# Transposes of q, k, p and x1 moved from TensorE to the DMA queue, in a transformer block with an LSTM

## The reference

```python
def cond(x, image):                      # causal attention, 16 heads of 16, one more key per sequence
    q, k, v = split(x @ c_attn_w + c_attn_b, 3)
    k = concat([image @ uk_w.T + uk_b, k]); v = concat([image @ uv_w.T + uv_b, v])
    p = softmax(where(causal, q @ k.T / sqrt(16), -10000) + mask)
    return (p @ v) @ c_proj_w + c_proj_b
def attn(y):                             # linear attention, relu on q and k, no softmax
    q, k, v = relu(y @ Wq.T + bq), relu(y @ Wk.T + bk), y @ Wv.T + bv
    out = (q @ (k.T @ v)) / max(q @ sum(k), 1e-6)
    return layernorm(out + y) * gamma + beta
x1 = x + attn(cond(x, image))
h  = lstm(x1, h0=image)                  # 64 steps over the tokens, 256 wide, gates 4 x 256
out = x1 + fp4_linear(silu(fp4_linear(h, w_gate)) * fp4_linear(h, w_up), w_down)
```

## Time and profile before

| | us |
|---|---|
| median of 3 runs | 1017.58 |
| lowest, highest | 1013.61, 1018.38 |
| the profiled execution | 1014.53 |
| its span, first to last instruction | 1012.4 |
| busy: TensorE, its weight loads | 866.5, 579.3 |
| busy: VectorE, ScalarE, GpSimd | 805.1, 495.7, 346.8 |

### The profile page before, as it was taken

The page is one execution under the profiler, slowest core; times in us unless marked ns, Lnnn a source line. Parts: engine busy times, 40 slices in busy tenths (PEclk is TensorE's granted clock), DMA queues, the critical chain, the costliest instruction groups (busy, mean ns, idle before and its releaser), DMA issues.

```text
span 1012.4 us, 27497 instructions
## 1 busy us (share of the span) xinstructions
PE 866.5 (86%) x9798; PEld 579.3 (57%) x9798; DVE 805.1 (80%) x2157; ACT 495.7 (49%) x1177; POOL 346.8 (34%) x436
## 2 busy tenths in 40 slices
PE   3359887988989898988977899999999999999984
PEld 1246655666666666666654565565665665666642
DVE  6388999778777877788764688888888888888884
ACT  2264656666676667666653333433343433333431
POOL 0053667555555556555642011111111111111111
PEclk9588999999999999999999999999999999999997
DMA  4600011011001110111010000000000000000001
GB/s 108 197 13 21 19 37 33 22 36 34 27 24 34 34 31 20 34 34 33 17 31 17 1 12 21 22 21 21 17 17 21 21 22 21 19 14 22 21 22 26
DMA packets 41239, 30.36 MB, mean 30 GB/s; under 512 B 12082, under 2 KB 40050, under 8 KB 41173
## 3 DMA queue, kind: packets, MB, share of 16 engines
q1 hardware_dynamic: 41172, 29.42, 10.3%
HBM read 20.87 MB, written 8.54 MB: 29 GB/s over the span
## 4 chain that ended last, share of the span: by engine, by line
PE 39%; DVE 23%; issue 13%; ACT 5%; POOL 2%; DVEq 1%; POOLq 0%; ACTq 0%
PE bank L713 14%; PE bank L882 8%; PE bank L981 6%; PE bank L871 6%; DVE hqT L1533 3%; PE bank L973 3%; ACT hqT L1183 2%; DVE kv_bd L1381 2%; DVE pT L458 2%; ACT qk L1054 1%; DVE h_value L170 1%; DVE qk L1375 1%; PE bank L718 1%; DVE prob L1323 1%; DVE v L1394 1%
## 5 line engine op out<-in xcount | busy, mean ns | idle before, releaser
L665 POOL TENSOR_TENSOR ffn_room<-h_value,h_scale 128x704 f32<-128x704 f32 x32 | 44.4, 1388 | 291.7 <-DVE h_value L171 291.7
L713 PE MATMUL bank<-gu,xqT 128*128 128x512 f16 (+1 forms) x576 | 128.2, 362 | 1.3 <-DVE xqT L1548 1.3
L613 POOL TENSOR_TENSOR p<-prob,p 128x520 f16<-128x520 f32 x64 | 80.5, 1258 | 68.4 <-ACT p L1065 68.3
L882 PE MATMUL bank<-wh,h 128*64 128x512 f16 x768 | 100.2, 385 | 3.5 <-ACT h L1158 2.1
L871 PE MATMUL bank<-wx,x1T 128*64 128x512 f16 x768 | 93.8, 379 | 0.9 <-DVE x1T L441 0.9
L772 PE MATMUL bank<-ident,p 128*65 128x128 f16 x1024 | 76.0, 223 | 16.5 <-ACT qT L1119 9.9
L981 PE MATMUL bank<-dn,hqT 128*128 128x256 f16 x576 | 70.3, 278 | 20.7 <-DVE hqT L1533 20.7
L1148 ACT ACTIVATE sig<-bank 128x256 f32<-128x256 f32 x64 | 24.8, 388 | 127.2 <-PE bank L882 126.6
L871 PEld LDWEIGHTS bank<-wx,x1T 128*64 128x64 f16 x768 | 78.9, 202 | 11.2 <-DVE x1T L441 1.2
L713 PEld LDWEIGHTS bank<-gu,xqT 128*128 128x128 f16 x576 | 53.7, 98 | 53.6 <-issue 9.9
L606 POOL TENSOR_TENSOR prob<-prob,row_max 128x520 f32<-128x520 f32 x64 | 68.5, 1089 | 37.0 <-DVE row_max L1331 36.8
(11 more groups left out here) (199 smaller groups left out, 2064.0 us busy)
## 6 DMA issues: line engine op xcount, KB each, us to landing
x_in<-in_x_columns SPq DMA_DIRECT2D x32, 128.0 KB, 2.2
x_res<-in_x SPq DMA_DIRECT2D x32, 128.0 KB, 2.1
x_rows<-x_rows_sb SPq DMA_DIRECT2D x32, 128.0 KB, 1.9
ffn_room<-x_rows SPq DMA_DIRECT2D x64, 64.0 KB, 2.2
out<-ffn_room SPq DMA_DIRECT2D x64, 64.0 KB, 2.0
mask_in<-in_mask_Bx1x1xS_ff SPq DMA_DIRECT2D x64, 16.0 KB, 2.4
x1T<-in_L_cond_Wx SPq DMA_DIRECT2D x1, 1024.0 KB, 6.5
x1T<-in_L_cond_Wh SPq DMA_DIRECT2D x1, 1024.0 KB, 8.5
```

The costliest lines, as they stand in the source:

```text
L613: pool.tensor_tensor(p16[:, 1, r, :], prob[:, r, :], p16[:, 0, r, :], ALU.subtract).then_inc(s["p_lo"], 1)
L665: pool.tensor_tensor(blocks(hq, FF), blocks(fp4_h.value, FF), spread(fp4_h.scale, FF), ALU.mult).then_inc(s["hq_ready"], 1)
L713: last = pe.matmul(dst, lhs(a, c), rhs(b, c), start=first and c == 0 and a == b, stop=c == C - 1 and (a, b) == parts3[-1], skip_group_chec ...
L882: last = pe.matmul(bank[e][B * h:B * h + B, :], h16[:, m, c, :], half_cols(wh16, a, c, h), start=False, stop=True, skip_group_check=True)
```

## The change

- q and k are transposed by two DMAs (64 rows x 2048 values each), p by two (128 rows x 1024 values, 8 heads each), x1 by one (128 rows x 512 values, high and low). The DMAs are issued by SyncE, in its list. The copies from PSUM behind TensorE's transposes go, and so do those transposes.
- p is laid out so that a head's 64 high and 64 low values become the 128 partitions of its transpose. v stands on the partitions twice, so one product gives high and low: 32 products in `attend` for 64. v is made twice by TensorE, for each sequence and each half of the partitions.
- The image key is left out of the transposed p. GpSimd multiplies its weight by the image's values (`image_part`), and VectorE adds that to the sums. The image's values come per tile as broadcast rows by two DMAs.
- All masks are loaded once, 1 MB, ahead of the first tile.
- x1's high and low parts are made from rows, by ScalarE and GpSimd, before they are transposed.
- `hold` is a wait as an instruction of its own, followed by the increment of a semaphore that nobody reads.
- The lists of all engines are reordered. Scores of the two halves use banks 0 to 3, one pair each.

The diff, cut to its core:

```diff
 def qkv(t):
...
-            after(pe, s["x1T_lo"], t.count(back=5))
-            lhs = lambda a, c: xT16[:, a, P * c:P * c + P]
-            for dst, lo, hi in ((bank[2], 0, 2 * D), (bank[1][:, 0:D], 2 * D, 3 * D)):
...
+            after(pe, s["masked"], t.count(2, 2, back=1))
+            bias(bank[2], "attn", 0, 2 * D)
+            product(bank[2], lambda a, c: xT16[:, a, P * c:P * c + P], lambda b, c: attn16[:, b, c, 0:2 * D], False)\
+                .then_inc(s["qk_ps"], 1)
+            row = bias_bf["attn"][:, None, 2 * D:3 * D].to_broadcast([96, 2, D])
+            pe.matmul(bank[3], ones_bf[:, :], row, start=True, stop=False, skip_group_check=True)
+            for h in range(2):
+                for c in range(C):
+                    for a, b in parts3:
+                        for copy in range(2):
+                            last = pe.matmul(bank[3][64 * copy:64 * copy + 64, D * h:D * h + D],
+                                             xT16[:, a, P * c + 64 * h:P * c + 64 * h + 64], attn16[:, b, c, 2 * D:3 * D],
+                                             start=False, stop=True, skip_group_check=True)
             last.then_inc(s["qkv_ps"], 1)
...
+        def scores(t, e):
             if e == 0:
+                hold(pe, qkT_in, t.count(per=32, nth=32), "pe_passed")
+                hold(pe, s["kimg_in"], t.count(), "pe_passed")
             else:
+                hold(pe, s["v_lo"], t.count(), "pe_passed")
...
+        def attend(t, e):
+            pe.wait_ge(pT_in[e], t.count(per=16, nth=16))
+            if e == 0:
+                pe.wait_ge(s["v_lo"], t.count())
+                after(pe, s["o_norm"], t.count(back=1))
+            for side in range(2):
                 for r in range(4):
                     for b in range(2):
                         q = slice(64 * b, 64 * b + 64)
+                        last = pe.matmul(o_ps[e][q, 2 * r + side, :, :], pT[:, 8 * e + 4 * side + r, q],
+                                         v16[:, t.parity, b, :, 8 * e + 2 * r + side, 0:HD + 1], start=True, stop=True,
+                                         skip_group_check=True)
             last.then_inc(s["pv_ps"], 1)
...
 TensorE, the new order of a step:
             if t4:
                 outer(t4)
...
+                rows_transpose(t3, bank[0], o_rows[:, :, :].rearrange("p h d -> p (h d)"), "o_norm", "onT_ps")
...
                 linear_out(t4)
...
+                project(t3)
             if t2:
                 attend(t2, 0)
+            if t3:
+                rows_transpose(t3, bank[6][:, D:2 * D], y_rows, "y_sb", "yT_ps")
+            if t1:
+                scores(t1, 0)
+            if t2:
                 attend(t2, 1)
             if t1:
                 scores(t1, 1)
             if t3:
                 linear_q(t3)
...
+    def hold(eng, sem, value, passed):
+        if isinstance(value, int) and value <= 0:
+            return
+        eng.wait_ge(sem, value)
+        eng.sem_inc(s[passed], 1)
...
 SyncE:
+        for b in range(2):
+            sp.dma_start(mask_in[64 * b:64 * b + 64, :, :], mask_sides[b].partition_broadcast(S)).then_inc(mask_loaded, 16)
...
+        def probs_turn(t, e):
+            hold(sp, s["p_lo"], t.count(e + 1, 2), "sp_passed")
+            hold(sp, s["pv_ps"], t.count(e + 1, 2, back=1), "sp_passed")
+            r = slice(8 * e, 8 * e + 8)
+            sp.dma_start_transpose(pT[:, r, :], p16[:, r].rearrange("p h i k -> p (h i k)")).then_inc(pT_in[e], 16)
...
+                hold(sp, s["img_part"], t1.count(2, 2, back=2), "sp_passed")
                 for b in range(2):
+                    row = vimg_dram[t1.number() * 2 + b]
+                    sp.dma_start(vimg_in[64 * b:64 * b + 64, q].rearrange("p h c -> p (h c)"), row.partition_broadcast(S))\
+                        .then_inc(vimg_loaded[q], 16)
                 if t1.loop is None and t1.b == 0:
                     late_loads()
+            if t2:
+                probs_turn(t2, 0)
+            if t1:
+                hold(sp, s["qk_split"], t1.count(2, 2), "sp_passed")
+                hold(sp, s["scores_ps"], t1.count(2, 2, back=1), "sp_passed")
+                for b in range(2):
+                    r = slice(64 * b, 64 * b + 64)
+                    sp.dma_start_transpose(qkT[:, b, :, 0:S], qk16[r].rearrange("p h s d -> p (h s d)")).then_inc(qkT_in, 16)
+            if t2:
+                probs_turn(t2, 1)
...
                 sp.dma_start(x1_tiles[t5.number()], x1_rows[:, :]).then_inc(s["x1_stored"], 16)
+                hold(sp, s["x1_lo"], t5.count(), "sp_passed")
+                sp.dma_start_transpose(x1T_all[:, :, :, bass.ds(t5.number() * 2, 2), :].rearrange("p i c b s -> p (i c) (b s)"),
+                                       x1_split[:, :, :].rearrange("p i d -> p (i d)")).then_inc(s["x1T_in"], 16)
...
 GpSimd:
+        def image_part(t, e):
+            pool.wait_ge(s["probs"], t.count(e + 1, 2))
...
+            weight = prob[:, 8 * e:8 * e + 8, S:KEYS].rearrange("p (s r) k -> p s r k", s=2)
+            pool.tensor_tensor(halves(o_img, e), halves(vimg_in[:, t.parity], e), weight.to_broadcast([P, 2, 4, HD + 1]),
+                               ALU.mult).then_inc(s["img_part"], 1)
...
+                pool.tensor_tensor(x1_split[:, 1, :], x1_rows[:, :], x1_split[:, 0, :], ALU.subtract).then_inc(s["x1_lo"], 1)
...
```

More of the change, by code:

```diff
@@ L42 @@
 SLOT = 32
-O_SLOTS = 3 * H // 4
+QK_RUN = 80
 FFC = -(-FF // P)
@@ L432, in program @@
     parts3 = ((0, 0), (0, 1), (1, 0))
-    def x1_part(eng, t, part):
-        src = bank[2][:, D:2 * D].rearrange("p (c n) -> p c n", c=C)
-        dst = [x1T16[i][:, :, bass.ds(t.number() * 2, 2), :].rearrange("p c b s -> p c (b s)") for i in range(part + 1)]
-        if part == 0:
-            last = eng.copy(dst[0], src)
-        else:
-            last = eng.tensor_tensor(dst[1], src, dst[0], ALU.subtract)
-        last.then_inc(s["x1T_lo" if part else "x1T_hi"], 1)
     def mask_count(t):
@@ L617, in step @@
             if t2:
+                shift(t2, 0)
                 shift(t2, 1)
+                image_part(t2, 0)
                 probs_lo(t2, 0)
[L620 to L625 removed]
             if t5:
@@ L638, in step @@
                 pool.tensor_tensor(xb_rows[:, :], x_res[:, :], beta_sb[:, :], ALU.add).then_inc(s["xb_ready"], 1)
+            if t1:
+                after(pool, s["scores_ps"], t1.count(2, 2, back=1))
+                pool.tensor_copy(qkT[:, :, H // 2:H, S:KEYS].rearrange("p b g o -> p g (b o)"),
+                                 kimgT[:, :, bass.ds(t1.number() * 2, 2)]).then_inc(s["kimg_in"], 1)
+            if t4:
                 if t4.loop is None and t4.b in SCALE_AT:
@@ L725, in qkv @@
                 pe.wait_ge(s["setup_done"], 1)
-            after(pe, s["x1T_lo"], t.count(back=5))
-            lhs = lambda a, c: xT16[:, a, P * c:P * c + P]
-            for dst, lo, hi in ((bank[2], 0, 2 * D), (bank[1][:, 0:D], 2 * D, 3 * D)):
-                if lo:
-                    after(pe, s["o_added"], t.count(back=2))
-                    after(pe, s["masked"], t.count(2, 2, back=1))
-                bias(dst, "attn", lo, hi)
-                last = product(dst, lhs, lambda b, c: attn16[:, b, c, lo:hi], False)
@@ L734, in qkv @@
-            last.then_inc(s["qkv_ps"], 1)
-        def qk_transpose(t):
-            rows = qk16[:, :, :, :].rearrange("p (g e) r d -> p g (e r d)", e=2)
-            for dst, g0, done in ((bank[0], 0, "qT_ps"), (bank[2], H // 2, "kT_ps")):
-                pe.wait_ge(s["qk_split"], t.count(2 if g0 else 1, 2))
-                for g in range(H // 2):
-                    last = pe.transpose(dst.bitcast(F16)[:, P * g:P * g + P], rows[:, g0 + g, :], ident16[:, :])
-                last.then_inc(s[done], 1)
@@ L761, in scores @@
             last.then_inc(s["scores_ps"], 1)
-        def probs_transpose(t, g):
-            pe.wait_ge(s["p_lo"], t.count(g // 2 + 1, 2))
-            if g < 2:
-                after(pe, pT_sb[g + 2], t.count(back=1))
-            if g >= 2:
-                pe.wait_ge(pT_sb[g - 2], t.count())
-            dst = bank[3 + g % 2].bitcast(F16)
-            for part in range(2):
-                for r in range(4):
-                    last = pe.transpose(dst[0:KEYS, P * (4 * part + r):P * (4 * part + r) + P],
-                                        p16[:, part, 4 * g + r, :], ident16[:, :])
-            last.then_inc(s["pT_ps"], 1)
@@ L811, in linear_q @@
             pe.wait_ge(s["yT_lo"], t.count())
+            after(pe, s["ctx_div"], t.count(back=1))
             for m in range(C):
@@ L1063, in probs_hi @@
             act.wait_ge(s["probs"], t.count(e + 1, 2))
-            after(act, s["pT_ps"], t.count(2 * e + 2, 4, back=1))
-            act.copy(p16[:, 0, r, :], prob[:, r, :]).then_inc(s["p_hi"], 1)
+            after(act, pT_in[e], t.count(per=16, nth=16, back=1))
+            act.copy(p16[:, r, 0, :], prob[:, r, 0:S]).then_inc(s["p_hi"], 1)
         def ffn_hi(t4, *places):
@@ L1320, in masked @@
```

(11 more changed lines are left out.)

307 lines of the change are left out of this document (114 added, 193 removed).

## The result

| | before | after |
|---|---|---|
| median of 3 runs, us | 1017.58 | 1083.18 |
| lowest, highest | 1013.61, 1018.38 | 1082.42, 1084.63 |
| the profiled execution, its span | 1014.53, 1012.4 | 1084.63, 1082.9 |
| busy: TensorE, its weight loads | 866.5, 579.3 | 843.2, 523.7 |
| busy: VectorE, ScalarE, GpSimd | 805.1, 495.7, 346.8 | 753.4, 406.0, 395.6 |

The time is 1.0658 of that before, with a 95% interval of 1.0633 to 1.0683: **65.6 us slower**, where I had forecast 55 less. First the page: the span, TensorE's granted clock in 40 slices, the packets, and the groups of scores and `attend` with the idle time ahead of them.

A forecast was written before the change was run, and what follows sets the result against it. It took a ring of waits, no full engine, to bound the first stage at 14.33 us a tile; the queue's ring of 12.4 saves 31 x (14.33 - 12.4) = 60, less 8: 1014.5 - 52 = 963 us, own range 925 to 1000.

The forecast's parts named there:

- The period before: First stage: 14.33 us a tile, a ring from linear_q through the copy of q and k and VectorE's list to yT.
- ring (c): Through the DMA queue: linear_q, q and k split, transposes, attend, scores, linear_q again; 8.9 + 3T, 12.4 us with separate waits.
- ring (a): VectorE's: TensorE to the end of qk 3.9, copy 0.8, VectorE's list 5.7; sum 10.4 us a tile.
- ring (b): GpSimd's: 9.8 us of work and 1.5 waiting from yT until the first maxima; 11.3 us a tile.
- The forecast ring: The deciding ring through the DMA queue, 12.4 us a tile, with 8.7 us of TensorE work and idling costed at nothing.
- 1.7 + 3T: Queue's part of the ring: 1.7 us fixed, plus data of q, k and half of p; 5.0 us.
- T: Data time of one 256 KB transposing DMA; taken as 1.1 us, with no transpose in the trace.
- The transposes' pieces: DMA transposes were taken to move in pieces of 256 bytes at 17 ns each.
- Rival 1: Transposes written in short pieces: T = 4.2, ring 21.5, 1245 us; decides from T = 1.8; chance 0.25 from 2.5 on.
- Rival 2: Issuing binds: each transpose holds SyncE for 2 us, ring 14.9 us, total 1041 us; chance 0.17.
- The work per tile: Work forecast in us: TensorE 8.7, VectorE 9.5, ScalarE 6.5, GpSimd 9.8.
- The ends: Cost outside the period: 5 us at the start for masks and late weight loads, 3 before the recurrent stage.

The follow-up runs named there:

- e3: GpSimd's two image multiplications left out of the kernel after: 1084.35 us, ratio 1.0651.
- e1: The kernel after, with 24 unread products a tile filling TensorE's waits: 1038.07 us, ratio 1.0198, period 14.31 us.
- e10: The kernel after with q and k transposed by TensorE again, y's rows held twice and yT's low part before the statistics: 967.41 us, ratio 0.9525.
- e4: The kernel after, with linear_q and linear_kv moved ahead of the first scores: 1122.74 us, ratio 1.103.
- e12: The kernel after with unread products in TensorE's waits and y's rows held twice, all transposes on the queue: 1026.46 us, ratio 1.0113.

## Why the prediction was wrong, point by point

- **The period before** and its ring were read right, and so was the form of the new one: ring (c) decided, over the queue, and neither ring (a) nor ring (b) (the chain after, and e3). It lacked the path over p's first half, which ends within 0.1 us of that over q and k.
- **The step that failed first**: "TensorE's granted clock was 1.00 in the 19 periods; it will idle more, and I cost that at nothing". The 4.30 us at 0.50 show otherwise: linear_q to the end of q and k took 6.13 us for 3.9. That is 2.2 of the 4.1 us a tile between 12.4 and 16.5, and e1 gave 2.17 back. The reason given, that this trace shows no other case, is wrong. It does, outside the 19 periods: the clock by slices on the page of the kernel before, and a stretch at its start (columns as in rows 2).

```profile
PEclk9588999999999999999999999999999999999997
```

```profile
50.00:100.00 50.00, 37.96 (x546) 27.54 (x545) 42.71 (x90) 28.17 (x52) 22.63 (x20) 0.81 0.07 18
```

TensorE was busy there for 0.76 of the time, and the clock was 0.81. The forecast ring had TensorE with 8.7 us of work in 12.4, a share of 0.70, and waiting right ahead of the longest products of the ring.
- **The term that was mis-sized**: 1.7 + 3T, 5.0 us, measured 7.12. I had set issues at 0.4 us as for a load of x and let them lie beside the data. They take 1.24 and 1.92, and p's second half can't be issued before them: 3.4 us of SyncE, then a landing of 3.72. But the larger part is T: 1.3 for p and 1.8 for q and for k make 4.9 where three times 1.1 made 3.3, so 1.6 of the 2.1. With the data moving all but without a gap, the longer issues may be an effect of the slow data and not a cause; no run tells these apart. This makes the other 2.1 us, of which 0.2 is offset by small terms.
- **The transposes' pieces** of 256 bytes, and the price of a piece (21 ns for 17), were about right. Rival 1's short pieces didn't come, but q and k, at 145 GB/s, reached the T of 1.8 from which it was to decide; with p at 1.3 the three make 4.9 us for its 5.4. By the Trainium skill (DMA: Bandwidth & Descriptors, Latency and other measured facts) a transposing DMA reaches 261 GB/s, measured in one kernel; the traces here have 210 with 128 source rows and 145 with 64, so the measurement decides against the figure. The 1309 ns of the Trainium skill for a block of 128x128 (VectorE: DVE Perf Modes, The three transpose paths) are not a pace: eight such blocks move in 1.3 to 1.8 us. They are close to the 1.2 to 1.3 us of an issue, which I hadn't thought to compare.
- **Rival 2, issuing binds,** came near with 1.25 to 1.9 us an issue for its 2 us, but in the period shown it was the data that had no gap, and its time of 1041 lacked the clock. With the clock restored, e1 is at 1038.07; that they agree so closely is luck in part, since the two add up other terms (14.9 us a tile there, 14.31 in e1).
- **The work per tile** of GpSimd and ScalarE came out as counted, VectorE's 0.7 above. TensorE's 8.7 was too low: e1 has 12.5 us at a clock of 1.00, of which the unread products are some 3.0, so 9.5 are left. The prices taken off overlap each other: the groups of rows 5 have 609 products of 220 ns in 44.4 us, so neighbours overlap by 0.15 us and not by 0.1, and taking a group away frees less than its busy time.
- **The ends**: 8.3 us more lie between the last load of x and the first product of the recurrent stage (78.1 us for 69.9), and 2.4 behind it, where I had 5 at the start and 3 at the end.
- **Rings (a) and (b)** at 10.4 and 11.3 were never reached. e10, without the queue in its chain, closes at 12.38 over VectorE; that the 0.68 us copy of kT is back explains part of the gap to 10.4, the rest I didn't take apart.

**What stays open.** In e10 two edits were made together (y's second buffer, and yT's low part ahead of the statistics); which carries more is open. So is what p on the queue would give alone, and what the changed lists cost without it. The ring of e4 was read from its chain and not tested. Why the steps ahead of the loop gained 12 us in e12 and nothing in e1 is not known.

## What to carry to other kernels

A transfer that takes work off an engine is paid in the ring that it enters: write that ring down with the queue's issue times and the time of the data for each shape (here 1.8 us for 256 KB from 64 rows, 1.3 from 128), and count what stands ahead of each transfer. Where an edit makes TensorE wait ahead of its long products, cost those products at its lower clock too (here 2.2 us a tile, as much as the mis-sized transfers), and try unread products or, better, the removal of the wait. Of a change that moves several operands, move only those whose landing no ring needs soon: with y held twice, p and x1 on the queue and q and k on TensorE gave 967 us, and all on the queue 1026, even with the clock restored by unread products.

## What the runs showed of the hardware

- A transposing DMA held SyncE for 1.2 to 1.3 us, the same for 128 and 256 KB, against 0.40 us for a plain load of 128 KB. It was 1.9 us right behind q's transpose: q and k together have a median of 1.6 and a longest of 3.4.
- It moved 256-byte pieces at about 210 GB/s from 128 source rows and at about 145 from 64. The distance of the target rows (80 or 128 values) changed nothing.
- It landed 2.5 us (x1), 3.4 us (p) and 4.4 us (q and k) after its issue, where a plain load of 128 KB took 2.1.
- With TensorE busy for 12.3 of 16.5 us a tile the granted clock was 0.81 in the loop; with 24 short unread products a tile it was 1.00, and the period 2.17 us shorter.
